# Gate's and up weights as half rows in 128 partitions, and the up weights' quantisation behind the third part of the first recurrence

## The chip, the core and the metric

The kernel runs on one core of one Trainium2 chip. The metric is the device time of one execution in microseconds (us). The core's engines run side by side, each through its own queue in order, and wait for one another by semaphores: PE (TensorE, matrix products and transposes by the identity), DVE (VectorE), ACT (ScalarE), POOL (GpSimd), and SP, which here only issues DMAs. TensorE works on data in SBUF (128 partitions) and writes to PSUM.

## The reference, cut to what matters

One layer of a language model over 16 sequences of 256 tokens, width 256, all in float32: a token embedding, an RWKV block (time mixing with a recurrence over tokens, then channel mixing), and a gated feed-forward part whose weights and activations are quantised to FP4 values in blocks of 16 and back.

```
h = (w0[x] @ w1) * (x != 0) * 16
y = layernorm(h)
k, v, r = (mixes of ln1(y) with its shift by one token) @ wk, wv, wr
wkv: per token  p = max(pp, u + k); out = (e^(pp-p) aa + e^(u+k-p) v) / (e^(pp-p) bb + e^(u+k-p)); state decays by w
x1 = y + (sigmoid(r) * wkv) @ wo;  x2 = x1 + sigmoid(..@ cwr) * (relu(..@ cwk)**2 @ cwv)
h = h + x2
n = fp4(layernorm(h))
fp4(x): per block of 16 along the last dim: scale = max|x| / 6, q = nearest of 0, .5, 1, 1.5, 2, 3, 4, 6, times sign and scale
h = h + fp4(silu(n @ fp4(w_gate).T) * (n @ fp4(w_up).T)) @ fp4(w_down).T
```

`w_gate` and `w_up` are 704 x 256, `w_down` is 256 x 704. They are quantised in the kernel, once, at its start.

## The kernel before

The 4096 tokens are cut into 8 chunks of 512. Each chunk goes through three stages, A (embedding, norm, k, v, r, the recurrence), B (attention output, channel mixing) and C (the quantised feed-forward part), and the chunks follow one another in a software pipeline. Its order is written by hand: the table `ORDER` holds for each engine the steps of one turn with a lag each (a step with lag n works on chunk t - n in turn t), and `walk` issues them in that order. Steps whose names begin with `w_` run only once, for the weights: `w_quant0`, `w_quant1`, `w_quant2` on VectorE quantise gate, up and down; `w_sq0` to `w_sq2` on ScalarE make the squares that each quantisation needs in its middle; `w_turn0` and so on transpose on TensorE and copy out on ScalarE (`up_hi`); `w_split0`, `w_split1` on VectorE make the remainder `up_lo`. The products with these weights take both.

A quantisation (`quantise`, lines 352 to 368) is seven stages, each on two parts n = 0, 1: the blocks' maximum, scale, reciprocal (352 to 356), the normalised data (358), two roundings by adding a large number that comes from ScalarE's square (362 and 365), and the product with the scale (368). ScalarE's squares (887) need stage four (358) and are waited for by the first rounding. The down weights stand in 128 partitions with 704 columns per part; gate and up stand in 88 partitions, `(j p) d -> p j d` with p = 88, 8 rows of 256 per partition and weight, so 1024 columns per part. The raw gate and up weights share `kkT`, which chunk 0's channel mixing writes only after both have been transposed. `square_w`, the room for the squares, lies in `xq_hi` and `xq_lo`.

Gate's, up's and down's weights and then `cwk` (to `mix2`, printed as `mix`) come by DMAs on SP's queue, issued in that order. ScalarE casts `cwk` (`w_key`, line 819).

The recurrence (`a_wkv1` to `a_wkv4`) goes between VectorE and ScalarE: part 1 (1005, 990, 1020) makes the running maximum from k; ScalarE's `a_wkv1` and `a_wkv2` make the exponentials (792); part 2 has the products with v and the scans (990, 1034, 1036); part 3 the numerator and denominator (990; the last writes `keep`); then ScalarE's `a_wkv3` takes the logarithm (`take<-keep`) and its exponential (`take<-take`), and part 4 on VectorE (990, 987, 990, 987) finishes and multiplies by r. The attention output (`b_out`, PE line 548 with `wo_s`) follows. ScalarE needs a table load (ACT_TABLE_LOAD) ahead of the logarithm, of the exponential behind it, and of the sigmoid for r.

Of the kernel before, what the change touches and what calls it, by code (L numbers as in the profile page):

```python
# [26 lines left out]
F32 = mybir.dt.float32  # L27
# [7 lines left out]
P = 128  # L35
SEQS, T = 16, 256
D = 256
# [6 lines left out]
GP = 88  # L44
GJ = INTER // GP
# [136 lines left out]
def build(nc, x, tok_w0, tok_w1, params, wk, wv, wr, wo, cwk, cwv, cwr, w_gate, w_up, w_down, out):  # L182
    out_tiles = out.rearrange("s (u p) d -> p (s u) d", p=P)

    with ExitStack() as ctx:
# [103 lines left out]
        raw_up = kkT[0:GP].rearrange("p k c -> p (k c)").rearrange("p (j d) -> p j d", d=D)  # L289
# [85 lines left out]
        def _(sp):  # L375
# [10 lines left out]
            for k, w in enumerate((w_gate, w_up)):  # L386
                sp.dma_start(raw_up[:, k * GJ:(k + 1) * GJ, :], w.rearrange("(j p) d -> p j d", p=GP)).then_inc(s_raw[k], 16)
# [94 lines left out]
        def _(pe):  # L482
# [166 lines left out]
            def turn_w(m):  # L649

                def step(_):
                    if m < 2:
                        pe.wait_ge(s_wq, QUANT * 2 * (m + 1))
                        for d in range(H):
                            if m:
                                pe.wait_ge(s_wc, d + 1)
                            for j in range(GJ):
                                mm = nc.tensor.transpose(psC[:, d, j // 4, (j % 4) * GP:(j % 4 + 1) * GP],
                                                         raw_up[:, m * GJ + j, d * P:(d + 1) * P], ident[0:GP, 0:GP])
                            mm.then_inc(s_wt, 1)  # L660
                        return
# [20 lines left out]
        def _(act):  # L682
# [195 lines left out]
            def square_of_w(k):  # L878
                def step(_):
                    for n in range(2):  # L880
                        act.wait_ge(s_wq, 2 * QUANT * k + 6 + n + 1)
                        if k < 2:
                            src = raw_up[:, 8 * k + 4 * n:8 * k + 4 * n + 4, :].rearrange("p j d -> p (j d)")
                            dst = square_w[n][0:GP]
                        else:
                            src, dst = raw_down[:, n, :], square_w[n][:, 0:INTER]
# [17 lines left out]
            def turn_w(m):  # L904
                def step(_):
                    for d in range(H):
                        act.wait_ge(s_wt, 2 * m + d + 1)
                        if m == 2:
                            turned(psC, d, downT[:, :, d * P:(d + 1) * P], s_wd)
                        else:  # L910
                            nc.scalar.copy(up_hi[:, m, d, :].rearrange("p (f n) -> p f n", f=2),
                                           psC[:, d, :, 0:INTER // 2]).then_inc(s_ws, 1)
# [14 lines left out]
        def _(dve):  # L927
# [239 lines left out]
            def quant_w(k):  # L1167

                def step(_):
                    dve.wait_ge(s_raw[k], 16)  # L1170
                    if k < 2:
                        parts = [part(n, raw_up[:, 8 * k + 4 * n:8 * k + 4 * n + 4, :].rearrange("p j d -> p (j d)"),
                                      square_w[n][0:GP], GP, NBW, scales_w) for n in range(2)]
# [5 lines left out]
            def split_w(m):  # L1179

                def step(_):
                    for d in range(H):
                        dve.wait_ge(s_wt, 2 * m + d + 1)
                        dve.wait_ge(s_ws, 2 * m + d + 1)
                        nc.vector.tensor_tensor(up_lo[:, m, d, :].rearrange("p (f n) -> p f n", f=2), psC[:, d, :, 0:INTER // 2],
                                                up_hi[:, m, d, :].bitcast(F32).rearrange("p (f n) -> p f n", f=2), ALU.subtract
# [44 lines left out]
```

## Time and profile before

| | |
|---|---|
| median of 3 runs | 785.88 us (785.11 to 786.6) |
| the profiled execution | 786.62 us, span 784.8 us |
| mean granted TensorE clock | 0.958 |
| PE busy | 698.4 us (89%) |
| DVE busy | 600.1 us (76%) |
| ACT busy | 512.1 us (65%) |
| POOL busy | 146.7 us (19%) |

The span runs from the first to the last instruction; the time of an execution lies a little above it. A busy time is the sum of an engine's instructions, whatever they were worth. The granted clock is a share of TensorE's full speed, 1.00 being 2.4 GHz and 0.50 being 1.2 GHz. In the timeline a row is a group of like instructions in a row on one engine: start, length of the group, engine and line, operation, written tile, read tiles, partitions x columns, their number, and in brackets how long the engine sat idle before and what ended that.

### The profile page before, as it was taken

What the parts mean: (1) busy time and instruction counts of PE and PEld (TensorE: products, weight loads), DVE (VectorE), ACT (ScalarE), POOL (GpSimd) and SP (SyncE); (2) the same over time, 40 slices, a digit from 0 to 9 for tenths busy, and PEclk for the clock granted to TensorE, in tenths of its full rate; (3) what the DMA queues carried; (4) which work ended last, traced back from release to release, by engine and by line L of the source; (5) the groups of instructions that cost most, each with busy time, mean ns of one, the idle gap of its engine ahead of it and who ended that gap; (6) DMA issues with size and microseconds to landing.
All of it is one profiled execution on the core that took longest, in us unless ns stands there. A gap on an engine that the chain in (4) does not pass through costs nothing.

```text
span 784.8 us, 9883 instructions
## 1 busy us (share of the span) xinstructions
PE 698.4 (89%) x3311; PEld 565.1 (72%) x3311; DVE 600.1 (76%) x1023; ACT 512.1 (65%) x889; POOL 146.7 (19%) x220
## 2 busy tenths in 40 slices
PE   4262799699999999999999999999999999699866
PEld 3231676589688977888688958897788768688664
DVE  0798745987798888788788778888878788863764
ACT  2448488578874888389757886588848974662221
POOL 2302230433023300421022302330141002200000
PEclk9676799899999999999999999999999999999999
DMA  3900000000010000100000001000010000000000
GB/s 122 255 16 27 1 28 1 28 1 28 1 41 14 27 1 14 41 1 27 14 30 13 28 14 28 15 28 0 25 30 1 1 14 15 1 0 14 14 1 28
DMA packets 11956, 19.34 MB, mean 25 GB/s; under 512 B 972, under 2 KB 9346, under 8 KB 11906
## 3 DMA queue, kind: packets, MB, share of 16 engines
q1 hardware_dynamic: 9302, 10.31, 4.4%
q0 software_dynamic: 2560, 8.39, 3.5%
q8 instruction: 27, 0.44, 0.2%
q14 instruction: 23, 0.19, 0.1%
q10 hardware_dynamic: 44, 0.01, 0.0%
HBM read 14.51 MB, written 4.19 MB: 24 GB/s over the span
## 4 chain that ended last, share of the span: by engine, by line
PE 69%; DVE 16%; ACT 6%; issue 6%; DMA 2%; POOL 0%; DVEq 0%; ACTq 0%; POOLq 0%; SPq 0%
PE psB L548 18%; PE psB L575 11%; PE psC L617 11%; PE psC L644 11%; PE psA L539 9%; PE psA L511 3%; PE psC L631 2%; ACT mix L798 2%; DVE top L352 1%; DVE mix L1084 1%; DMA rows<-L_tok_w,ids_now 1%; PE psB L521 1%; DMA kkT<-L_ffn_w_gate 1%; ACT take L792 1%; PE psA L499 1%
## 5 line engine op out<-in xcount | busy, mean ns | idle before, releaser
L548 PE MATMUL psB<-cwv_s,kkT 128*128 128x256 f32 x512 | 113.2, 379 | 0.0
L548 PEld LDWEIGHTS psB<-cwv_s,kkT 128*128 128x128 f32 x512 | 96.6, 190 | 16.1 <-issue 3.7
L431 POOL DMA_INDIRECT rows<-L_tok_w,ids_now x32 | 46.2, 1443 | 278.6 <-PE psA L499 266.9
L617 PE MATMUL psC<-up_hi,xq_hi 128*128 128x352 f32 x256 | 88.5, 346 | 9.0 <-DVE xq_lo L1196 8.0
L539 PE MATMUL psA<-mix,kvr_s 128*128 128x512 f32 x192 | 89.3, 611 | 6.4 <-ACT kT L768 6.4
L644 PE MATMUL psC<-downT,hqT 128*128 128x256 f32 (+1 forms) x384 | 95.0, 392 | 0.0
L644 PEld LDWEIGHTS psC<-downT,hqT 128*128 128x128 f32 (+1 forms) x384 | 68.7, 189 | 26.0 <-issue 18.8
L617 PE MATMUL psC<-up_hi,xq_lo 128*128 128x352 f32 x256 | 84.1, 329 | 0.0
L617 PE MATMUL psC<-up_lo,xq_hi 128*128 128x352 f32 x256 | 83.7, 327 | 0.0
L539 PEld LDWEIGHTS psA<-mix,kvr_s 128*128 128x128 f32 x192 | 36.9, 196 | 47.4 <-issue 46.2
L965 DVE SCALAR_TENSOR_TENSOR mix<-hT,rest,mix 128x512 f32<-128x512 f32 x80 | 54.3, 746 | 10.3 <-ACT mix L746 10.3
L511 PE MATMUL psA<-w_s,rowsT 128*128 128x256 f32 x256 | 61.6, 397 | 0.0
L617 PEld LDWEIGHTS psC<-up_hi,xq_hi 128*128 128x128 f32 x256 | 49.5, 193 | 11.6 <-DVE xq_lo L1196 9.0
L511 PEld LDWEIGHTS psA<-w_s,rowsT 128*128 128x128 f32 x256 | 50.7, 201 | 7.3
L575 PE MATMUL psB<-key_hi,cwk_hi 128*128 128x512 f32 x128 | 54.2, 424 | 1.9 <-ACT rr L837 1.9
L362 DVE SCALAR_TENSOR_TENSOR hq<-square,hq 128x704 f32<-128x704 f32 x32 | 28.6, 892 | 35.1 <-ACT square L875 35.1
L746 ACT ACTIVATE mix<-hT,par 128x512 f32<-128x512 f32 x80 | 51.0, 731 | 0.2
L575 PE MATMUL psB<-key_lo,cwk_hi 128*128 128x512 f32 x128 | 50.7, 396 | 0.0
L575 PE MATMUL psB<-key_hi,cwk_lo 128*128 128x512 f32 x128 | 50.6, 395 | 0.0
L617 PEld LDWEIGHTS psC<-up_hi,xq_lo 128*128 128x128 f32 x256 | 49.5, 193 | 0.8
L548 PE MATMUL psB<-wo_s,rT 128*128 128x256 f32 x128 | 34.5, 419 | 17.2 <-DVE rT L987 17.2
L617 PEld LDWEIGHTS psC<-up_lo,xq_hi 128*128 128x128 f32 x256 | 49.4, 193 | 0.0
(163 smaller groups left out, 1431.1 us busy)
## 6 DMA issues: line engine op xcount, KB each, us to landing
out<-h SPq DMA_DIRECT2D x16, 256.0 KB, 2.1
mix<-L_attn_cwk SPq DMA_DIRECT2D x1, 1024.0 KB, 13.8
cwv_s<-L_attn_cwv SPq DMA_DIRECT2D x1, 1024.0 KB, 15.8
kkT<-L_ffn_w_gate SPq DMA_DIRECT2D x1, 704.0 KB
kkT<-L_ffn_w_up SPq DMA_DIRECT2D x1, 704.0 KB
hqT<-L_ffn_w_down SPq DMA_DIRECT2D x1, 704.0 KB, 13.4
w_s<-L_tok_w SPq DMA_DIRECT2D x1, 512.0 KB, 4.0
rows<-L_tok_w,ids_now POOLq DMA_INDIRECT x32, 4.3
```

The lines of the kernel that those rows point to most:

```text
L362: op = nc.vector.scalar_tensor_tensor(out=data, in0=w.bitcast(F32), scalar=MAGIC, in1=data, op0=ALU.add, op1=ALU.add)
L431: pool.indirect_dma_start(rows[:, q, :], None, tok_w0, bass.IndirectOffsetOnAxis(ap=ids_now[:, s, t:t + 1], axis=0)).then_inc(rows_in[q], 16)
L511: mm = nc.tensor.matmul(psA[:, A.slot(f"e{j}"), q * D:(q + 1) * D], rowsT[:, q, k, :], w1_s[:, k, :], start=(k == 0), stop=(k == KE - 1))
L539: mm = nc.tensor.matmul(psA[:, A.slot(f"{name}{d}")], kvr_s[:, w, k, d * P:(d + 1) * P], mix[:, w, k].rearrange("p c t -> p (c t)"), start ...
L548: mm = nc.tensor.matmul(psB[:, B.slot(name), q * D:(q + 1) * D], lhsT[:, k, (2 * j + q) * P:(2 * j + q + 1) * P], weight[:, k, :], start=( ...
L575: mm = nc.tensor.matmul(psB[:, B.slot(f"kk{m}")], a[:, k, m * P:(m + 1) * P], b[:, k], start=(k == 0 and p == 0), stop=(k == H - 1 and p = ...
L617: mm = nc.tensor.matmul(psC[:, C.slot(name), f, 0:INTER // 2], a[:, k, t * P:(t + 1) * P], b[:, w, k, f * (INTER // 2):(f + 1) * (INTER // ...
L631: mm = nc.tensor.transpose(psC[0:n, C.slot(name), k // 4, (k % 4) * P:(k % 4 + 1) * P], hq[:, t, k * P:k * P + n], ident[:])
L644: mm = nc.tensor.matmul(psC[:, C.slot(name), 0, q * D:(q + 1) * D], hqT[0:n, q, k, :], downT[0:n, k, :], start=(k == 0), stop=(k == KI - 1))
L746: nc.scalar.activation(dst[:, w, d], src[:, d, :, 1:ROW], ACT.Identity, scale=col(m, d)).then_inc(sig.sem, 1)
L798: nc.scalar.activation(x1[:, t, :], x1[:, t, :], ACT.Identity, scale=sc_b[:, 1, t:t + 1], bias=sc_b[:, 3, t:t + 1]).then_inc(b_norm.sem, 1)
L965: nc.vector.scalar_tensor_tensor(out=dst[:, w, d], in0=src[:, d, :, 0:T], scalar=rest[:, PARAMS.index(m) - MIXES, d:d + 1], in1=dst[:, w, ...
```

## The change

Gate and up are read as half rows: the 704 rows of 256 become 1408 half rows of 128, of which each of 128 partitions holds 11 (`GJ = INTER * H // P`). A block of 16 never crosses a half row. A part of the quantisation is then 704 columns in 128 partitions, as it is for the down weights (`halves`). TensorE turns 8 half-row groups into the first bank pair of `psC` and 3 into the second; row and half alternate in the columns there, so the copy and the split read every second column (`turned_part`).

The steps `w_quant1` on VectorE and `w_sq1` on ScalarE move in the table.

```diff
-GP = 88
-GJ = INTER // GP
+GJ = INTER * H // P
...
     "act":
-        ("c_turn1", 1), ("a_cols", -1), ("c_sq2", 1), ("b_key1", 0), ("a_part", -1), ("w_sq1", -1), ("w_par", -2),
...
+        ("a_wkv2", -1), ("a_r", -1), ("w_sq1", -1), ("a_wkv3", -1), ("c_turn2", 1), ("w_turn2", 0), ("a_y", -1),
...
     "dve":
-        ("a_mix", 0), ("w_quant1", 0), ("c_up3", 2), ("c_quant3", 2), ("a_wkv1", 0), ("w_key", 0), ("c_down0", 2),
...
+        ("w_par", -2), ("a_wkv3", 0), ("w_quant1", 0), ("b_value0", 1), ("c_stat0", 1), ("a_wkv4", 0),
...
-        raw_up = kkT[0:GP].rearrange("p k c -> p (k c)").rearrange("p (j d) -> p j d", d=D)
+        raw_up = kkT[:].rearrange("p k c -> p (k c)")[:, 0:2 * GJ * P].rearrange("p (j d) -> p j d", d=P)
+
+        def halves(k, n):
+
+            return kkT[:].rearrange("p k c -> p (k c)")[:, (2 * k + n) * INTER:(2 * k + n + 1) * INTER]
+
+        def turned_part(d):
+
+            first, last = 8 * d * P // H, min(8 * d + 8, GJ) * P // H
+            return slice(first, last), psC[:, d].rearrange("p b n -> p (b n)")[:, 0:(last - first) * H].rearrange("p (n h) -> p h n", h=H)
...
-                sp.dma_start(raw_up[:, k * GJ:(k + 1) * GJ, :], w.rearrange("(j p) d -> p j d", p=GP)).then_inc(s_raw[k], 16)
+                sp.dma_start(raw_up[:, k * GJ:(k + 1) * GJ, :], w.rearrange("n (h d) -> (n h) d", h=H).rearrange("(j p) d -> p j d", p=P)).then_inc(s_raw[k], 16)
...
-                            for j in range(GJ):
-                                mm = nc.tensor.transpose(psC[:, d, j // 4, (j % 4) * GP:(j % 4 + 1) * GP],
-                                                         raw_up[:, m * GJ + j, d * P:(d + 1) * P], ident[0:GP, 0:GP])
+                            for j in range(8 * d, min(8 * d + 8, GJ)):
+                                mm = nc.tensor.transpose(psC[:, d, j % 8 // 4, (j % 4) * P:(j % 4 + 1) * P],
+                                                         raw_up[:, m * GJ + j, :], ident[:])
...
-                            nc.scalar.copy(up_hi[:, m, d, :].rearrange("p (f n) -> p f n", f=2),
-                                           psC[:, d, :, 0:INTER // 2]).then_inc(s_ws, 1)
+                            there, here = turned_part(d)
+                            nc.scalar.copy(up_hi[:, m, :, there], here).then_inc(s_ws, 1)
...
-                    if k < 2:
-                        parts = [part(n, raw_up[:, 8 * k + 4 * n:8 * k + 4 * n + 4, :].rearrange("p j d -> p (j d)"),
-                                      square_w[n][0:GP], GP, NBW, scales_w) for n in range(2)]
+                        parts = [part(n, halves(k, n), square_w[n][:, 0:INTER], P, NB, scales_w) for n in range(2)]
...
-                        nc.vector.tensor_tensor(up_lo[:, m, d, :].rearrange("p (f n) -> p f n", f=2), psC[:, d, :, 0:INTER // 2],
-                                                up_hi[:, m, d, :].bitcast(F32).rearrange("p (f n) -> p f n", f=2), ALU.subtract
+                        there, here = turned_part(d)
+                        nc.vector.tensor_tensor(up_lo[:, m, :, there], here, up_hi[:, m, :, there].bitcast(F32), ALU.subtract
```

What this does to the order in the queues is read best from the instructions themselves. First ScalarE, from the products that begin the mixes of chunk 0 (`mix<-hT,par`) to the exponential ahead of the recurrence's fourth part; before the change:

```order
L746 ACTIVATE mix<-hT,par 128x512 x6
L887 ACTIVATE xq_hi<-kkT 88x1024
L887 ACTIVATE xq_lo<-kkT 88x1024
L819 CAST cwk_hi<-mix 128x2048
L768 ACTIVATE kT<-psA 128x512 x2
...
L768 ACTIVATE rT<-psA 128x512 x2
L792 ACT_TABLE_LOAD
L792 ACTIVATE take<-keep 128x2x256 x2
L792 ACT_TABLE_LOAD
L792 ACTIVATE take<-take 128x2x256 x2
```

and of the changed kernel, whose lines are numbered some nine higher:

```order
L755 ACTIVATE mix<-hT,par 128x512 x6
L828 CAST cwk_hi<-mix 128x2048
L777 ACTIVATE kT<-psA 128x512 x2
...
L777 ACTIVATE rT<-psA 128x512 x2
L895 ACTIVATE xq_hi<-kkT 128x704
L895 ACTIVATE xq_lo<-kkT 128x704
L801 ACT_TABLE_LOAD
L801 ACTIVATE take<-keep 128x2x256 x2
L801 ACT_TABLE_LOAD
L801 ACTIVATE take<-take 128x2x256 x2
```

The up weights' squares went from ahead of the cast of the key weights to between the copies of r and the table load for the logarithm.

On VectorE the same stretch begins with the mixes of chunk 0 and ends with the recurrence's fourth part; before, the quantisation stands between the mixes and part 1:

```order
L965 SCALAR_TENSOR_TENSOR mix<-hT,rest,mix 128x512 x6
L352 TENSOR_REDUCE hq<-kkT 88x64 x2
L354 TENSOR_SCALAR hq<-hq 88x64 x2
...
L368 SCALAR_TENSOR_TENSOR kkT<-kkT,hq 88x1024 x2
L997 MEMSET top 128x4
L1005 SCALAR_TENSOR_TENSOR top<-decay,kT 128x256 x4
...
L990 TENSOR_TENSOR keep<-mix,take 128x2x256 x2
L990 TENSOR_TENSOR mix<-keep,take 128x512 x2
```

and of the changed kernel:

```order
L973 SCALAR_TENSOR_TENSOR mix<-hT,rest,mix 128x512 x6
L1005 MEMSET top 128x4
L1013 SCALAR_TENSOR_TENSOR top<-decay,kT 128x256 x4
...
L998 TENSOR_TENSOR keep<-mix,take 128x2x256 x2
L361 TENSOR_REDUCE hq<-kkT 128x44 x2
L363 TENSOR_SCALAR hq<-hq 128x44 x2
...
L377 SCALAR_TENSOR_TENSOR kkT<-kkT,hq 128x704 x2
L998 TENSOR_TENSOR mix<-keep,take 128x512 x2
```

It now stands between the denominator (`keep`, the end of part 3) and the first instruction of part 4 (`mix<-keep,take`).

## Rows read from the trace of the kernel before

**Rows 1.** Busy time, clock, DMA by stretch: us; PE, PEld, DVE, ACT, POOL busy; PEclk, share, GB/s.
```profile
200.00:300.00 100.00, 99.42 (x461) 77.97 (x460) 80.70 (x139) 74.75 (x130) 17.93 (x26) 1.00 0.06 17
```
**Rows 2.** Timeline, all engines, 21 to 46 us: start, length, engine, line, what.
```profile
26.41 2.34 DVE L352 TENSOR_REDUCE hq<-kkT 88x64 f32<-88x1024 f32 x2 [0.80 <-DMA kkT<-L_ffn_w_gate]
...
33.05 2.06 ACT L723 ACTIVATE kT<-h,sc_a 128x256 f32<-128x256 f32 x4
...
38.07 3.79 ACT L746 ACTIVATE mix<-hT,par 128x512 f32<-128x512 f32 x6
38.95 4.06 DVE L965 SCALAR_TENSOR_TENSOR mix<-hT,rest,mix 128x512 f32<-128x512 f32 x6
...
39.08 2.61 PE L658 MATMUL psC<-ident,kkT 88*128 88x88 f32 x16 [1.94 <-DVE kkT L368]
...
41.48 4.20 PE L539 MATMUL psA<-mix,kvr_s 128*128 128x512 f32 x8
```
**Rows 3.** Timeline, all engines, 42 to 60 us.
```profile
42.92 2.33 DVE L352 TENSOR_REDUCE hq<-kkT 88x64 f32<-88x1024 f32 x2
...
49.56 1.88 ACT L819 CAST cwk_hi<-mix 128x2048 fp32r<-128x2048 f32 x1
...
51.35 1.07 ACT L768 ACTIVATE kT<-psA 128x512 f32<-128x512 f32 x2
...
52.08 9.19 PE L539 MATMUL psA<-mix,kvr_s 128*128 128x512 f32 x16 [6.39 <-ACT kT L768]
...
58.50 1.34 ACT L792 ACTIVATE keep<-take,decay 128x512 f32<-128x512 f32 x2
```
**Rows 4.** Timeline, all engines, 66 to 76 us.
```profile
66.60 1.28 ACT L792 ACT_TABLE_LOAD   x1
...
70.83 1.28 DVE L990 TENSOR_TENSOR keep<-mix,take 128x512 f32<-128x512 f32 x2
71.54 1.23 ACT L792 ACTIVATE take<-keep 128x512 f32<-128x512 f32 x2 [3.66 <-DVE keep L990]
72.79 1.28 ACT L792 ACT_TABLE_LOAD   x1
...
74.75 1.29 DVE L990 TENSOR_TENSOR mix<-keep,take 128x512 f32<-128x512 f32 x2 [2.64 <-ACT take L792]
```
**Rows 5.** Timeline, the down weights' quantisation, 87 to 97 us.
```profile
87.82 1.65 DVE L352 TENSOR_REDUCE hq<-hqT 128x44 f32<-128x704 f32 x2
...
92.58 2.06 ACT L798 ACTIVATE mix<-mix,sc_b 128x256 f32<-128x256 f32 x4
...
95.20 1.69 DVE L368 SCALAR_TENSOR_TENSOR hqT<-hqT,hq 128x704 f32<-128x704 f32 x2
```
**Rows 6.** Timeline, the first casts of the turned weights and the attention's output.
```profile
78.05 1.39 ACT L911 CAST up_hi<-psC 128x704 fp32r<-128x704 f32 x2
...
79.91 5.50 PE L548 MATMUL psB<-wo_s,rT 128*128 128x256 f32 x16 [11.98 <-DVE rT L987]
```
**Rows 7.** Busy time, clock, DMA by stretch, columns as in rows 1.
```profile
20.50:22.50 2.00, 2.00 (x11) 1.71 (x9) 0.00 (x0) 0.00 (x0) 0.00 (x0) 1.00 0.64 158
...
34.00:39.00 5.00, 1.97 (x8) 1.57 (x8) 5.00 (x6) 3.60 (x7) 0.17 (x1) 0.50 0.92 325
39.00:42.50 3.50, 3.42 (x18) 2.90 (x19) 3.50 (x7) 2.86 (x5) 0.00 (x0) 0.50 0.31 107
43.00:46.00 3.00, 2.68 (x7) 0.90 (x5) 3.00 (x7) 0.00 (x0) 0.00 (x0) 1.00 0.00 0
52.00:56.00 4.00, 3.92 (x5) 1.85 (x6) 4.00 (x6) 0.55 (x2) 0.00 (x0) 0.50 0.00 0
```
**Rows 8.** Timeline, k's products of chunk 1 at full clock.
```profile
118.11 3.59 PE L539 MATMUL psA<-mix,kvr_s 128*128 128x512 f32 x8
```
**Rows 9.** Timeline, SP's queue: the issue of the key weights' DMA.
```profile
21.83 1.21 SPq L389 DMA_DIRECT2D mix<-L_attn_cwk  x1
```
**Rows 10.** DMA issues of the page: the key weights, KB, us to landing.
```profile
mix<-L_attn_cwk SPq DMA_DIRECT2D x1, 1024.0 KB, 13.8
```

More of the change, by code:

```diff
@@ L882, in step @@
                         if k < 2:
-                            src = raw_up[:, 8 * k + 4 * n:8 * k + 4 * n + 4, :].rearrange("p j d -> p (j d)")
-                            dst = square_w[n][0:GP]
+                            src, dst = halves(k, n), square_w[n][:, 0:INTER]
                         else:
```

10 rows, old and new, of the table ORDER are left out of this document.

## The prediction

> **What bounds the kernel now.** I read the busy time by stretches first. From 200 us on TensorE is busy for 99.4 of 100 us at full clock [rows 1], and the change touches nothing there. What it touches lies in the first 107 us, before the first wide products of chunk 0, and there the chain of waits runs through single instructions. So I went down the timeline of that head, engine by engine. The reader is to see three stations in it.
>
> First, the gate weights' quantisation on VectorE starts at 26.41 when its DMA lands. ScalarE's norm of chunk 0 stands behind the two squares of it and starts at 33.05; everything up to the mixes (38.07 on ScalarE, 38.95 to 43.01 on VectorE) hangs on that norm [rows 2]. Second, VectorE then takes the up weights from 42.92, and ScalarE's queue holds their squares too, so that the cast of the key weights (49.56) and the copy of k (51.35) come only behind them; TensorE, out of k's products at 45.68, gets the v products at 52.08, and the recurrence's first exponential part starts at 58.50 [rows 3]. Third, the recurrence's third part ends on VectorE at 72.11, the logarithm starts at 71.54 with its table already there (loaded at 66.60), and the fourth part starts at 74.75 [rows 4]. Behind it everything to 107 us waits for it in turn.
>
> **The change, part by part.** The profiled execution took 786.62 us around a span of 784.8; the median of the three timed runs is 785.88, so 0.74 less. I work in the profile's times and take 0.74 off at the end.
>
> *Price of a quantisation.* Today 88 partitions with 1024 columns, then 128 with 704. That second form is in the trace: it is the down weights' quantisation. It runs from 87.82 to 96.89, that is 9.07, and ScalarE is free for its next item 4.76 after the start (92.58) [rows 5]. Gate's runs from 26.41 to 39.0 (12.6) and frees ScalarE after 6.64 [rows 2]. So 3.5 less on VectorE per weight, 1.88 less for ScalarE.
>
> *Start of the first.* I leave it at 26.41. VectorE waited 0.80 for the landing [rows 2], with nothing else to do, so a faster one gains at most 0.8. The half rows double the packets (1408 in place of 704). For a bound from the other side I take all the time from 20.5, where gate's packets run, to 26.41, that is 5.9: if every half row cost as much as a row does today, 88 per engine on 16 engines against 64 on 11 would make 8.1 of it, 2.2 later. Today's share of DMA while gate's packets run is 0.64, close to 11 of 16 engines [rows 7]. The Trainium skill (DMA: Bandwidth & Descriptors, "Why a DMA increments its semaphore by 16 and not by 1") says that a transfer is spread over the largest number up to 16 that divides the outer dimension: 11 for 88 partitions, 16 for 128. By that rule and the bytes alone, gate would land 5.9 x 5/16 = 1.8 earlier, of which the statistics let 0.8 through and the forecast would be 780.5. The window's share agrees with the rule on today's 11 engines.
>
> *From there to k.* Norm at 26.41 + 4.76 = 31.17, which is 1.88 earlier; the chain of turning, affine and mixes moves with it: ScalarE's products end at 41.86 - 1.88 = 39.98, VectorE's mixes run 37.07 to 41.1 (VectorE itself is free at 35.5). TensorE turns the gate weights from 35.5 in 11 transposes of 128 columns for 16 of 88, 2.7 for 2.61 (1408 columns either way) [rows 2], done by 38.2; k's products start when the first two mixes are there, 38.5, against 41.48.
>
> *The removed block.* ScalarE goes from the products straight to the cast of the key weights (1.88 us [rows 3]), 39.98 to 41.86, and copies k. The copy of the k half that v's bank waits for is done by 42.5. How long k's products take depends on the clock. At full clock the eight passes take 3.59 [rows 8], at half twice that less the tail of the last one, some 6.9. In both half-clock stretches of the trace that begin with work after a rest the clock is still 0.50 some 3.5 and 4 us in [rows 7]. If it rises a good microsecond after k's start as today, k ends at 42.7, v at 46.2, its copy at 46.8: the exponentials start 11.7 earlier. If it takes 3.8 us, they end 1.1 later: 10.6. I take 11.2. (All at half: 45.4, 52.3, 52.9: only 5.6; that is the end kept for the range.) Nothing else holds that stretch: VectorE's scans can start at 42.5 and its share of the key weights fits before the first take, as now.
>
> *The third part and the block that is put behind it.* It ends at 72.11 - 11.2 = 60.9. Then VectorE runs the up weights' quantisation: 60.9 + 9.07 = 69.97. On ScalarE its squares stand ahead of the logarithm, and behind them stands the table load, which today is hidden under VectorE's work. So ScalarE: squares done at 60.9 + 4.76 = 65.66, load 1.28 [rows 4], logarithm at 66.94, and from there to the fourth part 74.75 - 71.54 = 3.21 [rows 4]: 70.15. The two meet within 0.2; the later decides: 70.15 in place of 74.75, **4.6 earlier**. In other words the move earns 11.2 and gives back 6.6. Of the block's 9.07 the pause that VectorE has there today (72.11 to 74.75) covers 2.64; 6.4 lie on the path, and ScalarE's way adds 0.2.
> Against this stands the Trainium skill (ScalarE: Activation LUTs, "What ACT_TABLE_LOAD costs"): each switch costs 1.28 for the load and 1.38 for a drain. By that rule the fourth part would start at 71.5 and 1.4 of the gain would go. The trace speaks against it here: the load at 72.79 ends at 74.07, and the fourth part, which needs a whole exponential of 0.6 behind it, starts at 74.75 [rows 4].
>
> *Casts and splits.* The four casts of 704 columns become two pairs of 1024 and 384, read from PSUM two apart. Same columns, same count; 0.75 each today [rows 6]. The first pair (gate) has room: what VectorE does behind that split needs the first half of the attention's output, which TensorE starts at 79.91 and takes 5.5 over [rows 6]. The second pair (up) lies on ScalarE's path ahead of the gate sigmoid. Contiguous reads are all that the trace shows: 0 if spacing is free, +1.4 if a column costs double. I take 0, the row that there is, and keep the other end.
>
> *Carried to the end.* From the fourth part on, order and durations are the same on every engine, and no transfer is late (the DMA share is 0.31 in 39 to 42.5 and 0.00 after [rows 7]; the up weights are asked for at 60.9). So the 4.6 should arrive whole: 786.62 - 4.6 - 0.74 = **781.3 us**.
>
> **Rivals.**
> 1. *More is gained.* Gate lands at 25.6 (-0.8), the clock rises early (-0.5), and a phase at half clock later in the head is spared (TensorE's work from 79.91 takes 5.5 us for columns that full clock does in 3.6 [rows 6, 8]: up to -1.9). For: TensorE works almost without rest from 33 us. Against: but for eight transposes it rests from 51 to 75 afterwards, longer than now. Time down to 778.1, about 779.5 in the middle. Chance 0.15.
> 2. *Less is gained.* Packets cost by number (+2.2), or spaced PSUM reads cost double (+1.4). Either gives 782.7 to 783.5; both 784.9. For: the doubled packet count, and 158 GB/s at a share of 0.64 in gate's window against 325 GB/s at 0.92 later, where the long rows of the key weights run [rows 7]: packets do cost more per byte when short. Against: five more engines share them. Chance 0.15.
> 3. *Nothing is gained*, since a transfer or a queue that I took as covered binds the recurrence's start; the gain of 11.2 is then 6.6 or less. For: the key weights' DMA (behind gate and up on the same queue) must land before 40; today it takes 13.8 from its issue at 21.83, so 35.6 [rows 9, 10], and is not asked for until 49.56. Against: 4.4 us of room. Time 784.5 to 787. Chance 0.05.
> 4. *Slower: TensorE stays at half clock.* From 33 us its work comes in pieces with rests between; should the clock not rise before v is done, the exponentials start only 5.6 earlier instead of 11.2. The block behind the third part then costs its 6.6 all the same: 1.0 late. If the attention output's products stay at half too, 6.9 in place of 5.5, that is 1.4 more: +2.4, 788.3. It decides from a start less than 6.6 earlier than now. Against: the clock rose in the middle of k's products even after a rest of 2 us. Chance 0.05.
> That the change doesn't do what it says I exclude by the order of instructions: the block stands behind the third part on VectorE and behind r's copies on ScalarE.
>
> **How the numbers follow.** Forecast 0.60, rivals 0.15, 0.15, 0.05, 0.05. A difference below 0.2% (1.6 us) can't be told from none: faster means below 784.3. Forecast and rival 1 are faster, of rival 2 nearly all (0.13 of 0.15): 0.88. The same: 0.02 of rival 2, the most of rival 3 (0.04) and 0.01 of the others, 0.07. Slower: 0.05. The forecast's own bounds are -0.8 and +2.2 at the landing and 0.6 either way at the clock. 778.8 to 784.2 holds it, and most of rivals 1 and 2, and leaves out about 0.17.
>
> **What the new profile would show.** Gate's quantisation: 9.1 long, start between 25.6 and 28. Norm 4.8 behind its start. Exponentials' start near 47.3. Third part's end near 61, then the quantisation on VectorE, then the table load directly behind the squares and the fourth part at about 70.2, with both engines arriving within 0.3. First attention product at about 75.3 for 79.91, first key product 4.6 earlier, and the same distance at 200 us and at the end. I would be wrong if the exponentials start after 50, if a rest stands ahead of the cast of the key weights, or if the distance at 75 us is not the distance at 200 us.

## The result and the profile after

The changed kernel takes 777.14 us (median of 4 runs, 776.9 to 777.46), the kernel before, run beside it, 786.24 (4 runs, 785.11 to 787.42): ratio 0.9884, 95% interval 0.9867 to 0.9901. That is faster, as forecast, but by 9.1 us where 4.6 was forecast, and below the range. The profiled execution takes 776.9 around a span of 775.0, with a mean granted TensorE clock of 0.968; before it was 786.62, 784.8 and 0.958. Two executions of the later experiments, of 1819.73 and 936.23 us, where the others of the same kernels take 777 to 790, are left out of every figure.

I read the new trace at the stations of the prediction. First the head, up to the exponentials (columns as in [rows 2]: start, length, engine, line, what); it answers to [rows 2, 3]:

```profile
25.31 1.65 DVE L361 TENSOR_REDUCE hq<-kkT 128x44 f32<-128x704 f32 x2
...
30.07 2.06 ACT L732 ACTIVATE kT<-h,sc_a 128x256 f32<-128x256 f32 x4
...
35.08 3.79 ACT L755 ACTIVATE mix<-hT,par 128x512 f32<-128x512 f32 x6
...
37.30 3.70 PE L548 MATMUL psA<-mix,kvr_s 128*128 128x512 f32 x8 [0.65 <-DVE mix L973]
...
41.30 7.11 PE L548 MATMUL psA<-mix,kvr_s 128*128 128x512 f32 x16 [0.29 <-ACT kT L777]
...
45.50 1.32 ACT L801 ACTIVATE keep<-take,decay 128x512 f32<-128x512 f32 x2
```

Gate's quantisation starts 1.1 earlier and no longer waits for a DMA. The norm follows 4.76 behind its start and ScalarE's products 9.77 behind it, where the working had 4.76 and, as a first step, 33.05 + 5.02 - 1.88 - 26.41 = 9.78. The exponentials start 13.0 earlier than before: 1.1 of that is gate's earlier start, 11.9 its shorter quantisation and the removed block, together with the clock.

Next the third part and the block behind it; it answers to [rows 4]:

```profile
58.19 1.28 DVE L998 TENSOR_TENSOR keep<-mix,take 128x512 f32<-128x512 f32 x2
59.39 1.66 DVE L361 TENSOR_REDUCE hq<-kkT 128x44 f32<-128x704 f32 x2
...
62.68 0.79 ACT L895 ACTIVATE xq_hi<-kkT 128x704 fp32r<-128x704 f32 x1 [9.12 <-DVE kkT L367]
...
64.28 1.28 ACT L801 ACT_TABLE_LOAD   x1
...
65.58 1.15 ACT L801 ACTIVATE take<-keep 128x512 f32<-128x512 f32 x2
...
68.04 1.15 ACT L801 ACTIVATE take<-take 128x512 f32<-128x512 f32 x2
68.70 1.29 DVE L998 TENSOR_TENSOR mix<-keep,take 128x512 f32<-128x512 f32 x2 [0.23 <-ACT take L801]
```

The third part ends at 59.47. From there to the fourth part 9.23 pass, forecast 9.25; ScalarE is 0.23 later than VectorE. The fourth part starts at 68.70 for 74.75, which is 6.05 earlier. The ledger to here: forecast 4.6, plus 1.1 at the start, plus 0.7 between there and the exponentials (11.9 for 11.2), less 0.36 by which the stretch from the exponentials to the third part's end grew (13.61 before, 13.97 after).

Then the distance grows. Before the change, the transposes of the second norm and the embedding products of chunk 1, on the timeline at 88 to 108 us:

```profile
94.69 1.97 PE L521 MATMUL psB<-ident,mix 128*128 128x128 f32 x8 [2.91 <-ACT mix L798]
...
106.72 1.09 ACT L837 ACTIVATE rr<-psB 128x512 f32<-128x512 f32 x2
```

and the same place of the changed kernel:

```profile
73.87 5.28 PE L557 MATMUL psB<-wo_s,rT 128*128 128x256 f32 x16 [18.71 <-DVE rT L995]
...
86.31 2.06 ACT L807 ACTIVATE mix<-mix,sc_b 128x256 f32<-128x256 f32 x4
...
88.43 1.09 PE L530 MATMUL psB<-ident,mix 128*128 128x128 f32 x8 [2.93 <-ACT mix L807]
...
97.70 1.09 ACT L846 ACTIVATE rr<-psB 128x512 f32<-128x512 f32 x2
```

TensorE rests 2.9 us in both, and the items are the same. But its transposes take 1.97 before and 1.09 after. The sixteen products behind them (L511, L520) take 5.70 before and 3.62 after. The windows say why (columns as in [rows 1]; the granted clock is the third number from the end). Before:

```profile
92.00:94.00 2.00, 0.00 (x0) 0.00 (x0) 2.00 (x3) 2.00 (x4) 0.00 (x0) 0.96 0.00 0
94.00:100.00 6.00, 5.31 (x17) 4.59 (x18) 4.54 (x7) 5.55 (x10) 0.00 (x0) 0.50 0.00 0
735.00:739.00 4.00, 3.52 (x12) 3.52 (x13) 2.91 (x6) 1.24 (x3) 0.00 (x0) 0.57 0.19 66
```

and after:

```profile
20.50:22.50 2.00, 2.00 (x10) 1.52 (x8) 0.00 (x0) 0.00 (x0) 0.00 (x0) 1.00 1.16 328
...
85.50:88.40 2.90, 0.00 (x0) 0.00 (x0) 2.76 (x5) 2.90 (x7) 0.00 (x0) 1.00 0.00 0
88.40:93.00 4.60, 4.55 (x24) 3.79 (x24) 3.68 (x6) 4.49 (x8) 0.00 (x0) 1.00 0.00 0
726.00:730.00 4.00, 3.54 (x22) 3.54 (x23) 2.91 (x6) 1.87 (x4) 0.00 (x0) 1.00 0.19 64
```

In the kernel before the clock falls to half (1.2 GHz) at the end of the rest and stays there for some 6 us; in this execution of the changed one it stays at 2.4 GHz. The gate sigmoid (`rr<-psB`, behind a table load) starts 9.02 earlier: 6.05 of the fourth part, 0.22 more at the norm (the attention's products take 5.28 for 5.50), 2.75 behind it. From there the distance is rigid; the same line of a late chunk, before and after:

```profile
686.60 1.09 ACT L837 ACTIVATE rr<-psB 128x512 f32<-128x512 f32 x2
```
```profile
677.58 1.09 ACT L846 ACTIVATE rr<-psB 128x512 f32<-128x512 f32 x2
```

which is 9.02 again. The last 0.8 comes at the tail, where the same stretch (735 to 739 before, 726 to 730 after) runs at 0.57 before and 1.00 after. So of the 9.8 us of span 6.05 were gained up to the fourth part, and 3.8 behind it, where queues and waits are the same and TensorE's clock differs.

### The profile page after: what moved, and what is told of

The parts are those of the page before. It is cut to its first block, busy times and chain, and to the rows that moved or that the text cites. A ratio compares the mean times of both kernels' runs of the same rounds, so it can differ in the third digit from the quotient of the medians.

```text
span 775.0 us, 9863 instructions
## 1 busy us (share of the span) xinstructions
PE 693.1 (89%) x3301; PEld 561.0 (72%) x3301; DVE 593.0 (77%) x1023; ACT 510.4 (66%) x889; POOL 145.7 (19%) x220
## 4 chain that ended last, share of the span: by engine, by line
PE 70%; DVE 13%; ACT 9%; issue 6%; DMA 1%; DVEq 0%; ACTq 0%; POOL 0%; POOLq 0%
PE psB L557 18%; PE psB L584 12%; PE psC L653 11%; PE psC L626 11%; PE psA L548 9%; PE psA L520 4%; PE psC L640 2%; ACT mix L807 2%; DVE top L361 1%; DVE mix L1092 1%; PE psA L508 1%; PE psA L530 1%; ACT take L801 1%; DVE top L959 1%; PE psB L530 1%
## 5 line engine op out<-in xcount | busy, mean ns | idle before, releaser
L440 POOL DMA_INDIRECT rows<-L_tok_w,ids_now x32 | 42.6, 1331 | 264.0 <-PE psA L508 252.4
L548 PE MATMUL psA<-mix,kvr_s 128*128 128x512 f32 x192 | 86.8, 596 | 0.9 <-DVE mix L973 0.7
L520 PE MATMUL psA<-w_s,rowsT 128*128 128x256 f32 x256 | 59.8, 388 | 0.0
L520 PEld LDWEIGHTS psA<-w_s,rowsT 128*128 128x128 f32 x256 | 49.3, 196 | 6.7
```

The source lines that it names most:

```text
L440: pool.indirect_dma_start(rows[:, q, :], None, tok_w0, bass.IndirectOffsetOnAxis(ap=ids_now[:, s, t:t + 1], axis=0)).then_inc(rows_in[q], 16)
L520: mm = nc.tensor.matmul(psA[:, A.slot(f"e{j}"), q * D:(q + 1) * D], rowsT[:, q, k, :], w1_s[:, k, :], start=(k == 0), stop=(k == KE - 1))
L548: mm = nc.tensor.matmul(psA[:, A.slot(f"{name}{d}")], kvr_s[:, w, k, d * P:(d + 1) * P], mix[:, w, k].rearrange("p c t -> p (c t)"), start ...
```

## The experiments

The experiments ran on three chips, each beside the kernel before on the same chip. A diff is against the changed kernel unless the text says otherwise. In some kernels one item's transposes are issued several times into the same place, as filler; no kernel leaves work out.

**The layout alone.** The changed kernel with the order of before on ScalarE and VectorE:

```
-        ("a_wkv2", -1), ("a_r", -1), ("w_sq1", -1), ("a_wkv3", -1), ...
+        ("a_part", -1), ("w_sq1", -1), ("w_par", -2), ...
-        ("w_par", -2), ("a_wkv3", 0), ("w_quant1", 0), ("b_value0", 1), ...
+        ("a_mix", 0), ("w_quant1", 0), ("c_up3", 2), ...
```

> The half rows in 128 partitions with the order of the kernel before: the up weights' quantisation stays between the mixes and the first recurrence. Theory A (the layout carries the gain, the move gives back what it earns): gate lands at 25.3 and its quantisation is 3.5 shorter, so the mixes end 3.0 earlier (40.0); the second quantisation ends at 49.1 instead of 55.5, the exponentials start near 52.2 (6.3 earlier), the fourth part of the recurrence near 68.4, also 6.3 earlier, as early as in the changed kernel (68.7). Time near the changed kernel's 777 us if the clock stays up around 90 us, 780 if it falls there. Rival B (the move behind the third part carries most of it, as my forecast had it): the fourth part near 71.5, time 782 to 783.

Measured: 782.31 us, ratio 0.9926 (0.9897 to 0.9956). The seven runs fall in two groups: 777.56, 777.59 and 777.75 at a mean clock of 0.968, 782.31 to 784.85 at 0.952 to 0.956. The profile fell in the first group:

```profile
47.53 8.55 PE L548 MATMUL psA<-mix,kvr_s 128*128 128x512 f32 x16 [6.12 <-ACT kT L777]
53.18 1.32 ACT L801 ACTIVATE keep<-take,decay 128x512 f32<-128x512 f32 x2
...
69.42 1.29 DVE L998 TENSOR_TENSOR mix<-keep,take 128x512 f32<-128x512 f32 x2 [2.64 <-ACT take L801]
```

The layout brings the fourth part 5.33 of the 6.05 by itself. The block in its old place makes the exponentials 7.7 later than in the changed kernel; the block in its new place costs that back. Counted from gate's start (25.71 here, 25.31 there) the move is worth 43.71 - 43.39 = 0.3 us. At the same mean clock of 0.968 the times say the same: 777.56 to 777.75 for the layout alone, 776.9 to 777.38 for the five such runs of the changed kernel.

**The move alone.** The kernel before with the changed kernel's order on both engines (the reverse of the diff above):

> The order of the changed kernel with the weights in 88 partitions as before. Theory A: the exponentials start 8.8 earlier (49.7), the third part ends near 63.3, but the quantisation of 12.6 us behind it ends at 75.9, so the fourth part starts 1.1 LATER than before (74.75): 786 to 788 us, no gain at all. Rival B (the move earns more than it gives back): fourth part at 71 or earlier, 782 us.

Measured: 788.99 us, ratio 1.0025 (1.0009 to 1.0041): slower, by a quarter of a per cent. Its timeline:

```profile
50.09 1.32 ACT L792 ACTIVATE keep<-take,decay 128x512 f32<-128x512 f32 x2
...
76.47 0.68 DVE L990 TENSOR_TENSOR mix<-keep,take 128x512 f32<-128x512 f32 x1
```

The exponentials come 8.4 earlier, but the long form behind the third part takes 12.45 (64.02 to 76.47), where before 2.64 passed. From gate's start the fourth part is at 50.24, before at 48.34 [rows 2, 4]: 1.9 late. So the prediction's "the move earns 11.2 and gives back 6.6" doesn't hold for the move by itself: alone it earns 8.4 at the exponentials and gives back more. What is left over at the fourth part is the layout's.

**The clock at the second norm.** The kernel before with the up weights' 16 transposes issued three times, which fills TensorE ahead of the rest (90.2 to 94.0) and changes no data:

```
-                            for j in range(GJ):
+                            for j in [j for _ in range(3 if m else 1) for j in range(GJ)]:
```

> The kernel before, with the up weights' 16 transposes done three times over on TensorE (the same values into the same place), which fills TensorE's rest from 91.8 to 94.7. Theory C (2.7 us of the change's gain are a spared fall of TensorE's clock in that rest): the granted clock stays 1.00 there, the eight transposes and sixteen products behind it take 4.7 for 7.5, the gate sigmoid comes 2.7 earlier, and the time is 783.5. Rival D (the clock has nothing to do with it, or another wait takes its place at once): 786.

Measured: 785.82 us, ratio 0.9975 (0.9958 to 0.9993). Windows and timeline:

```profile
94.00:100.00 6.00, 4.57 (x25) 3.79 (x24) 5.09 (x8) 5.89 (x11) 0.00 (x0) 1.00 0.01 3
```
```profile
94.52 1.09 PE L521 MATMUL psB<-ident,mix 128*128 128x128 f32 x8 [0.50 <-ACT mix L798]
...
103.79 1.09 ACT L837 ACTIVATE rr<-psB 128x512 f32<-128x512 f32 x2
```

Without the rest there is no fall, and the sigmoid starts 2.93 earlier, 0.18 of it already at the norm. From the norm to the sigmoid it is 11.39 for 14.14, the 2.75 of the changed kernel to the digit. At the end only 1.0 of it is left, and the time came out as rival D had it. The distance is still 3.7 in the last stretch but one; then TensorE rests 3.06 us in both kernels, and this execution goes on at half clock where the kernel before had 1.00. VectorE's last wait for TensorE, before and here, and the clock in it here:

```profile
781.50 0.69 DVE L1163 TENSOR_TENSOR h<-h,psC 128x512 f32<-128x512 f32 x1 [6.80 <-PE psC L644]
```
```profile
780.51 0.69 DVE L1163 TENSOR_TENSOR h<-h,psC 128x512 f32<-128x512 f32 x1 [9.50 <-PE psC L644]
```
```profile
772.00:774.00 2.00, 2.00 (x8) 1.70 (x7) 0.00 (x0) 0.90 (x3) 0.00 (x0) 0.50 0.36 122
```

That is 2.7 us, as much as the second norm had given.

**The other side.** The changed kernel with the up weights' transposes behind chunk 1's embedding products, so that TensorE rests 4.1 us instead of 2.9:

```
-        ("c_up0", 2), ("c_cols1", 2), ("a_turn1", 0), ("w_turn1", 1), ("b_cols", 1), ("a_emb1", 0), ("c_up1", 2),
+        ("c_up0", 2), ("c_cols1", 2), ("a_turn1", 0), ("b_cols", 1), ("a_emb1", 0), ("w_turn1", 1), ("c_up1", 2),
```

> The changed kernel with the up weights' transposes moved on TensorE from ahead of the attention's transposes (84.1 to 85.5) to behind the second embedding product, so that TensorE rests 4.1 instead of 2.9 us before 88.4. Nothing waits for them earlier. Theory C: the clock falls in that rest to 0.50 and the gate sigmoid comes 2.7 later: 779.8. Rival D: 777.1 as the changed kernel.

Measured: 780.92 us, ratio 0.993 (0.9911 to 0.9949). The clock fell (0.57 in 90 to 94 us), and the sigmoid starts at 100.56, 2.9 later than in the changed kernel:

```profile
73.73 6.75 PE L557 MATMUL psB<-wo_s,rT 128*128 128x256 f32 x16 [18.66 <-DVE rT L995]
...
89.76 1.63 PE L530 MATMUL psB<-ident,mix 128*128 128x128 f32 x8 [4.13 <-ACT mix L807]
```

1.3 of that stands at the norm already (87.65 for 86.31), and comes from the attention's products: 6.75 for the 5.28 of the changed kernel, at a place that the edit doesn't touch. So the fall behind the rest costs at most 1.5 here, not 2.7, and one profile of a kernel doesn't fix what its clock does. That asked for the next run.

**The changed kernel again**, on another chip.

> The changed kernel once more, beside the layout alone, to see how its executions spread. Theory C (part of the gain is a clock that stays up in TensorE's rest of 2.9 us at 85 to 88 us, which a later or earlier start may lose): some executions near 777 at a granted clock of 0.968, and others 3 to 5 us longer at 0.955, as the layout alone had. Rival F (moving the block behind the third part makes the high clock certain): all executions near 777.

Measured: 779.4 us, ratio 0.9899 (0.9872 to 0.9926). By run, time and mean clock: 777.25 at 0.968, 777.3 at 0.968, 778.21 at 0.966, 780.6 at 0.956, 780.67 at 0.956, 783.29 at 0.952. The profile is the one of 780.6:

```profile
68.48 1.29 DVE L998 TENSOR_TENSOR mix<-keep,take 128x512 f32<-128x512 f32 x2 [0.23 <-ACT take L801]
...
73.64 6.34 PE L557 MATMUL psB<-wo_s,rT 128*128 128x256 f32 x16 [18.70 <-DVE rT L995]
...
89.27 1.97 PE L530 MATMUL psB<-ident,mix 128*128 128x128 f32 x8 [2.93 <-ACT mix L807]
...
100.03 1.09 ACT L846 ACTIVATE rr<-psB 128x512 f32<-128x512 f32 x2
```
```profile
86.50:89.00 2.50, 0.00 (x0) 0.00 (x0) 2.44 (x4) 2.50 (x5) 0.00 (x0) 1.00 0.00 0
89.50:92.50 3.00, 3.00 (x12) 2.73 (x12) 1.96 (x3) 2.55 (x5) 0.00 (x0) 0.50 0.00 0
```

The fourth part is where it was (43.39 behind gate's start, as in the first profile). The same 2.93 of rest is there. But here the clock fell, the transposes take 1.97, and the sigmoid starts 2.3 later (2.55 against the fourth part's start). Of the 2.55, 1.06 stands at the norm already, since the attention's products take 6.34 for 5.28; the fall behind the rest costs 1.49, as it lasts a shorter time than in the kernel before. Another 1.0 is lost in the next chunk, by 175 us, and 0.3 at the end. Same program, same queues, 3.7 us of span: this shows that the clock, and no wait, makes the difference behind the fourth part.

**The changed kernel with the filler** (its 11 transposes of the up weights three times):

```
-                            for j in range(8 * d, min(8 * d + 8, GJ)):
+                            for j in [j for _ in range(3 if m else 1) for j in range(8 * d, min(8 * d + 8, GJ))]:
```

> The changed kernel with the up weights' 11 transposes done three times over, which fills TensorE's rest before the attention's transposes but for some 0.7 us. Theory C: the clock stays 1.00 in every execution there; the gate sigmoid at 97.7 as in the changed kernel's profile, and fewer executions above 778, median 777 or a little less. Rival: a spread as in the changed kernel.

Measured: 778.8 us, ratio 0.9899 (0.988 to 0.9918), runs from 776.97 (clock 0.968) to 781.41 (0.958). The profile, of the fastest run, has the sigmoid at 97.85. Against the 779.4 of the unfilled kernel on the same chip it can't be told apart, so the median of 777 or less that I expected didn't come. So either this place is not where most executions lose, or the filler doesn't always hold; which of the two is open.

**The layout alone, again**, on a third chip and in nine runs, since three of the first seven had the high clock.

> The layout alone once more, for more executions of it. Theory A: its fourth part starts within 0.4 of the changed kernel's when counted from the start of gate's quantisation (43.7 against 43.4), and its executions at a granted clock of 0.966 and more lie within 0.6 us of the changed kernel's at that clock (777.3). Rival B: 2 us or more above them.

Measured: 783.22 us (781.7 to 785.09), ratio 0.9953 (0.9935 to 0.9971), clocks 0.952 to 0.960. Timeline and windows of its profile:

```profile
46.97 10.07 PE L548 MATMUL psA<-mix,kvr_s 128*128 128x512 f32 x16 [6.12 <-ACT kT L777]
54.15 1.32 ACT L801 ACTIVATE keep<-take,decay 128x512 f32<-128x512 f32 x2
...
70.38 1.29 DVE L998 TENSOR_TENSOR mix<-keep,take 128x512 f32<-128x512 f32 x2 [2.64 <-ACT take L801]
```
```profile
46.00:52.00 6.00, 5.03 (x6) 2.19 (x7) 6.00 (x11) 1.91 (x4) 0.00 (x0) 0.51 0.00 0
```

The fourth part stands 45.23 behind gate's start (25.15), against 43.71 in the first profile and 43.39 in the changed kernel; I had expected it within 0.4 of the latter. Here is what the move can do on top of the layout. With the block in its old place TensorE waits 6.12 us between k's and v's products, and the v products start at half clock, for a longer time in this execution than in the other. With the block moved, v follows k within 0.3 us, in the changed kernel at full clock: 7.11 for 10.07 and 8.55. By these profiles the move is worth 0.3 to 1.8 us at the fourth part. But the moved block doesn't make the full clock sure either. The kernel with the squares behind the logarithm (below) has the changed kernel's head up to the exponentials, and in its execution k's products began at half clock: the 24 products of k and v take 12.22, and the exponentials

```profile
46.68 1.32 ACT L801 ACTIVATE keep<-take,decay 128x512 f32<-128x512 f32 x2
```

stand 21.32 behind gate's start (25.36), for 20.19 in the changed kernel. That is 1.1 of the at most 1.8. So what the move is worth beyond 0.3 is not settled by one profile of each. Over both chips the layout alone has 16 runs, 3 at 0.966 or more, the changed kernel 10 runs, 7 of them so. The kernel before has none in some 50.

**Packets or engines.** Gate's landing: the kernel before with each row of gate and up fetched in two pieces of 512 bytes, still from 88 partitions:

```
-                sp.dma_start(raw_up[:, k * GJ:(k + 1) * GJ, :], w.rearrange("(j p) d -> p j d", p=GP)).then_inc(s_raw[k], 16)
+                for h in range(H):
+                    sp.dma_start(raw_up[:, k * GJ:(k + 1) * GJ, h * P:(h + 1) * P],
+                                 w.rearrange("(j p) d -> p j d", p=GP)[:, :, h * P:(h + 1) * P]).then_inc(s_raw[k], 16)
```

> The kernel before with gate's and up weights read in pieces of 512 bytes, still into 88 partitions (two DMAs for each weight). It tells packet size from number of engines. Theory H (the earlier landing of the changed kernel comes from 16 engines for 11; the packets of half a row cost about half): gate lands within 1 us of 26.4. Rival I (packets cost by number): gate lands 3 us or more later, and VectorE's first quantisation starts near 29.5.

One execution, 788.63 us at clock 0.948. Its queue and VectorE:

```profile
18.72 0.87 SPq L388 DMA_DIRECT2D kkT<-L_ffn_w_gate  x2
...
25.76 2.34 DVE L352 TENSOR_REDUCE hq<-kkT 88x64 f32<-88x1024 f32 x2 [0.18 <-DMA kkT<-L_ffn_w_gate]
```

Twice the packets on the same engines land 7.0 us after the issue, where whole rows took 7.66 in the profile of before (issued at 18.75, landed at 26.41 [rows 2]), 7.55 in the kernel with the move alone and 7.22 in the kernel before with the filler. Halving the packet costs nothing measurable here. In the changed kernel gate lands 4.9 us after its issue, as its page says:

```profile
kkT<-L_ffn_w_gate SPq DMA_DIRECT2D x1, 704.0 KB, 4.9
```

and the share of the DMA engines in 20.5 to 22.5 us is 1.16 at 328 GB/s, for 0.64 at 158 [rows 7]. At the same packet size the landing takes 4.9 for 7.0, which is 0.70; 11/16 is 0.69. (The profile's share passes 1 here, so it is no count of engines.) With the packets out, the number of engines is the reason that is left for the landing. This is what the Trainium skill says (DMA: Bandwidth & Descriptors, "Why a DMA increments its semaphore by 16 and not by 1"): a transfer takes the largest number of engines up to 16 that divides its outer dimension, so 16 for 128 partitions and 11 for 88. The ratio of the landings agrees.

**What sets the fourth part.** The changed kernel with the up weights' squares behind the recurrence's exponential on ScalarE, so that the logarithm needn't wait for them:

```
-        ("a_wkv2", -1), ("a_r", -1), ("w_sq1", -1), ("a_wkv3", -1), ("c_turn2", 1), ("w_turn2", 0), ("a_y", -1),
+        ("a_wkv2", -1), ("a_r", -1), ("a_wkv3", -1), ("w_sq1", -1), ("c_turn2", 1), ("w_turn2", 0), ("a_y", -1),
```

> The changed kernel with the up weights' squares on ScalarE behind the logarithm and its exponential instead of ahead of them. It tells which engine sets the start of the recurrence's fourth part. In the changed kernel the third part ends 9.23 before it. Theory J (VectorE's own nine microseconds of quantisation set it, and ScalarE's squares, table load, logarithm and exponential happen to take as long): the logarithm's table is loaded under other work, ScalarE is through with the exponential 3.9 after the third part's end, and yet the fourth part starts 9.3 to 9.8 after it, because the squares come some 0.4 to 0.7 later to VectorE's roundings. Rival K (ScalarE's row of squares, table load and logarithm sets it): the fourth part starts 9.07 or less after the third part's end.

One execution, 781.38 us at clock 0.960:

```profile
60.04 1.23 ACT L801 ACTIVATE take<-keep 128x512 f32<-128x512 f32 x2 [3.99 <-DVE keep L998]
...
69.52 1.29 DVE L998 TENSOR_TENSOR mix<-keep,take 128x512 f32<-128x512 f32 x2
```

The third part ends at 60.61 and the fourth starts 8.91 behind it, without a wait, for 9.23 in the changed kernel. So ScalarE's row (squares, table load, logarithm, load, exponential) sets the changed kernel, VectorE's own work would be through 0.3 earlier, and the prediction's "the two meet within 0.2" holds nearly.

**A version that beats both.** If what counts is the block on the path, it belongs where VectorE works off the path. The up weights' quantisation takes the place of the down weights' one (behind `b_x1`), the down weights' goes behind the split of chunk 1, the transposes follow, the squares on ScalarE move with them, and a fourfold `a_turn1` of chunk 1 fills TensorE's rest (VectorE's part of the diff):

```
-        ("w_par", -2), ("a_wkv3", 0), ("w_quant1", 0), ("b_value0", 1), ...
+        ("w_par", -2), ("a_wkv3", 0), ("b_value0", 1), ...
-        ("b_x1", 0), ("w_quant2", 0), ("c_norm1", 1), ...
+        ("b_x1", 0), ("w_quant1", 0), ("c_norm1", 1), ...
-        ("w_split1", 1), ("c_quant2", 2),
+        ("w_split1", 1), ("w_quant2", 1), ("c_quant2", 2),
```

> The changed layout with the up weights' quantisation put further back, behind the attention output's sum and statistics (where the down weights' stood), and the down weights' behind the up weights' split, in VectorE's rest before chunk 1's mixes; TensorE's rest before the attention's transposes is filled with repeated transposes of chunk 1's rows. Nothing then stands between the recurrence's third and fourth part. Theory A (the move behind the third part gives back 6.6 of what it earns): the fourth part starts near 62.1 instead of 68.7, the gate sigmoid near 91, and the time is 770 to 771. Rival G (the end is set by VectorE's sum of work in the head, so the block costs its 9 us wherever it stands): 775 to 778.

Measured: 776.35 us (773.57 to 777.29), ratio 0.9855 (0.9833 to 0.9877); the changed kernel, run beside it, has 779.4 and 0.9899. Its fourth part and sigmoid:

```profile
63.39 0.69 DVE L998 TENSOR_TENSOR mix<-keep,take 128x512 f32<-128x512 f32 x1 [2.64 <-ACT take L801]
...
92.41 1.08 ACT L846 ACTIVATE rr<-psB 128x512 f32<-128x512 f32 x2
93.36 1.67 DVE L361 TENSOR_REDUCE hq<-hqT 128x44 f32<-128x704 f32 x2
```

Both places are 5.3 earlier than in the changed kernel. At the logarithm of chunk 1 4.1 of it is left (129.83 for 133.91), as the down weights' quantisation, started at 93.36, stands ahead of chunk 1's norm and mixes. At 674 us 3.1 is left, and at the end of this execution nothing (span 775.3 for 775.0): from 758 to 768 us it ran at a granted clock of 0.66. So the 770 to 771 us that I expected aren't reached, and the time lies where the rival had it, but the two places show that the block costs less at its new place, and what eats the gain is in part the clock.

## Why the prediction was wrong

*Right.* The path was the right one, and most terms of the sum came out. Gate's quantisation frees ScalarE after 4.76, forecast 4.76. The block behind the third part costs 9.23, forecast 9.25, with ScalarE last. Where the table load stands bare, the logarithm starts right behind its 1.28 (64.28 to 65.58), so that no drain shows, as the prediction read from [rows 4]. Casts and splits cost what they cost before: 1.39 for 1408 columns and two apart [rows 6], so that the spaced reads of PSUM, half of rival 2, are free. The packets, its other half, are too. (Rival 3's time doesn't follow from its text: a gain of 6.6 for 11.2 leaves nothing at the fourth part, 785.9 and not 784.5.)

*Start of the first.* The step left it at 26.41 and the bounds allowed 0.8 for the landing; 1.1 was measured (0.8 for the landing, 0.3 since the head before it ran earlier in this execution; the layout-only profiles have 25.71 and 25.15). The prediction had a row that said 11 of 16 engines and a rule that agreed with it, and took zero because of a bound for packets that no row bore out. The packet run shows that this bound was empty. The share of 0.64 was a weak row as well: two executions with the same 88 partitions have 0.75 and 0.89 in that window.

*The removed block.* 11.2 was taken, with bounds of 0.6 either way; net of gate's earlier start 11.9 was measured. The clock was up at about 36, when TensorE was still turning the gate weights, and not a microsecond into k's products: k's products took 3.70.

*Carried to the end.* This step failed most and put the time outside the range: "the 4.6 should arrive whole". At the fourth part 6.05 had been gained, at the gate sigmoid 9.0, at the end 9.8. The prediction looked at transfers and order behind the fourth part, found them equal, and concluded that the durations are equal too. They were not: the profile of before held a fall of the clock at 94 us, within the stretch that moves, which I had not looked for, and another at 735. Rival 1 had the right idea, "a phase at half clock later in the head is spared", but named the attention's products (5.50 before, 5.28 after, so nearly nothing was spared there), not the second norm; it had a chance of 0.15 and was bounded at 1.9. That the first four runs all had the high clock is luck: 3 of the 6 later runs of the same program, at 780.6 to 783.3, lie inside the range.

*Shown and not shown.* Shown: the layout brings 5.3 of the 6.05 at the fourth part and about half of the time (4.7 and 3.3 us in the medians beside the kernel before, ratios 0.9926 and 0.9953, for 9.1 and 7.7 of the whole change); the move without the layout is slower (1.0025); a fall of the clock in the second norm's rest costs 2.75 in the kernel before and 1.5 in the changed one; with the block moved, the rest of 6.12 ahead of the v products is gone. Argued only: that the move is therefore what gives the changed kernel the high clock in 7 of 10 runs against 3 of 16; these runs come from different chips. The medians, 777.4 over 10 runs and 782.8 over 16, differ by more than the 0.3 to 1.8 at the fourth part explains, and the profiles show the rest as clock at places further down, in the layout alone and in the changed kernel alike. Open: why a rest of 2.9 us lets the clock fall in one execution and not in another of the same program. Since the changed kernel takes 777.3 or 780.6 by its clock alone, the 9.1 of the first comparison is at its favourable end; 7.7 (787.07 to 779.4) is what the runs on the second chip show.

## What to carry to other kernels

Where TensorE works in pieces, look up the granted clock in each of its stretches before saying that a distance is carried whole: a few us earlier or later can spare or cost a stretch at half clock, here 1.5 to 2.75 us for one, up to more than half the forecast gain. Take the work out of the critical row first (here the layout: 3.5 us per weight), and move it only then: the same move lost 1.9 us at the fourth part with the long form and won 0.3 with the short one, and up to 1.8 where the clock helped. Judge changes below 1% over several runs on more than one chip, with the mean clock of each run beside its time.

## What the runs showed of the hardware

- One program takes between 777.25 and 783.29 us on one chip, and the mean granted clock goes with it (0.968 and 0.952); the same 2.93 us rest of TensorE ends at 1.00 in one execution and at 0.50 in another. The Trainium skill (TensorE: Matmul & The Clock Gate, "What's actually happening") says that the cold start of one kernel varies from run to run; the traces here show such a variation in the middle of a kernel too.
- The cost of a fall depends on how long it lasts: behind the same rest 2.75 us in the kernel before, 1.5 in the changed one; behind a rest of 3.06 us at the end of the program, 2.7 in one execution and none in another.
- A 704 KB transfer into 88 partitions takes 7.2 to 7.7 us from issue to landing in rows of 1 KB, 7.0 in pieces of 512 bytes, and 4.9 into 128 partitions.
- A read of PSUM in fp32 with a stride of two costs what a contiguous one does: 1.39 us for 1408 columns on ScalarE, 1.68 on VectorE.
